# Two scatters a step instead of three while attention drains on GpSimd

## The reference

```
x = x + linear_attention(norm(x))      # 16 heads of 8, rotary
x = x + ffn(norm(x))                   # first mixture of experts
x = x + log_attention(norm(x))         # 16 heads of 8, causal
x = x + ffn(norm(x))                   # second mixture, same weights

log_attention:  L = q k^T / sqrt(8);  agg = sum_k(exp(clip(q ky^T / sqrt(8))) * mask)
                w = softplus(log(|L| + eps) - log(agg + eps)) * mask
                out = (w / (sum_k w + eps)) v @ w_proj^T
ffn:            shared expert on every token, plus the best 2 of 8 routed experts
                by sigmoid(x @ router + bias), weighted by the two normalised scores
```

## Time and profile before

| | us |
|---|---|
| median of 3 runs | 1026.67 (1026.3 to 1032.23) |
| the profiled execution | 1028.98 |
| its span | 1027.1 |
| busy in the span: PE / DVE / ACT / POOL | 819.4 / 735.8 / 568.5 / 586.9 |
| instructions of PE / DVE / ACT / POOL | 6459 / 1506 / 805 / 815 |
| mean granted clock of TensorE | 0.908 |

### The profile page before, as it was taken

One profiled execution on the slowest core, in us unless ns is written; L12 is line 12 of the kernel. 1 busy time (PEld: TensorE's weight loads), 2 busy tenths in 40 slices (PEclk: granted clock), 3 DMA queues, 4 the chain that ended last, 5 costly groups with the idle time before them and its releaser, 6 DMA issues. The chain is left out here.

```text
span 1027.1 us, 19542 instructions
## 1 busy us (share of the span) xinstructions
PE 819.4 (80%) x6459; PEld 545.3 (53%) x6459; DVE 735.8 (72%) x1506; ACT 568.5 (55%) x805; POOL 586.9 (57%) x815
## 2 busy tenths in 40 slices
PE   3887577899986787888888888979796588899890
PEld 2666566799984333333333333333342256799890
DVE  3888745455563658899999998989789646555574
ACT  1454152133334667989898989998763242233230
POOL 2343486881383666666644444455326877788884
PEclk9999588999997878999999999999877688999996
DMA  9990012123338477584737474732210021132444
GB/s 273 300 131 1 16 39 70 54 81 114 101 84 242 124 197 220 150 227 118 234 108 215 116 208 121 224 106 55 70 42 24 32 75 39 40 102 84 132 135 122
DMA packets 114401, 124.00 MB, mean 121 GB/s; under 512 B 13328, under 2 KB 76560, under 8 KB 114176
## 3 DMA queue, kind: packets, MB, share of 16 engines
q1 hardware_dynamic: 96512, 100.80, 36.2%
q0 software_dynamic: 8416, 17.29, 5.4%
q10 hardware_dynamic: 9376, 4.65, 1.6%
HBM read 59.97 MB, written 62.72 MB: 119 GB/s over the span
## 5 line engine op out<-in xcount | busy, mean ns | idle before, releaser
L2070 DVE TENSOR_SCALAR ring_b<-psum 128x1024 int32<-128x1024 int32 x160 | 194.2, 1216 | 24.0 <-PE psum L1765 20.8
L1930 ACT ACTIVATE ring_a<-psum 128x1024 f32<-128x1024 f32 x160 | 162.4, 1021 | 51.0 <-PE psum L1765 45.7
L1936 ACT ACTIVATE ring_b<-ring_b 128x1024 f32<-128x1024 f32 x160 | 168.7, 1055 | 36.5 <-DVE ring_b L2070 36.1
L2198 POOL TENSOR_SCALAR_AFFINE_SELECT ring_b<-ring_b 128x512 f32<-128x512 f32 (+1 forms) x112 | 80.1, 728 | 171.6 <-ACT ring_b L1936 170.9
L1765 PE MATMUL psum<-stacks 32*128 32x128 f32 (+3 forms) x1024 | 98.9, 385 | 66.2 <-DVE ring_b L2070 36.8
L1765 PEld LDWEIGHTS psum<-stacks 32*128 32x128 f32 x1024 | 56.9, 193 | 173.5 <-ACT ring_a L1930 76.6
L2062 DVE TENSOR_SCALAR ring_a<-ring_a 128x1024 f32<-128x1024 f32 x160 | 119.4, 751 | 16.8 <-ACT ring_a L1930 15.0
L949 ACT ACTIVATE ring_b<-psum 128x512 f32<-128x512 f32 x72 | 42.6, 591 | 114.0 <-PE psum L834 88.0
L1818 PE MATMUL psum<-ring_b,values 128*32 128x256 f32 (+3 forms) x1024 | 94.2, 478 | 8.6 <-POOL ring_b L2198 8.6
L1797 PE MATMUL psum<-ring_a,ones_s 128*32 128x256 f32 (+3 forms) x1024 | 92.3, 469 | 9.8 <-POOL ring_a L2198 9.8
L1092 POOL DMA_INDIRECT r_rows<-y_sorted,rows_of x64 | 67.1, 1048 | 51.3 <-DMA y_sorted<-y_out 39.2
(11 more groups left out here) (220 smaller groups left out, 1484.1 us busy)
## 6 DMA issues: line engine op xcount, KB each, us to landing
stack_q<-parts SPq DMA_DIRECT2D x32, 256.0 KB
stack_ky<-parts SPq DMA_DIRECT2D x32, 256.0 KB
stacks<-stack_q SPq DMA_DIRECT2D x64, 128.0 KB
stacks<-stack_ky SPq DMA_DIRECT2D x64, 128.0 KB
stack_k<-parts SPq DMA_DIRECT2D x32, 256.0 KB
stacks<-stack_k SPq DMA_DIRECT2D x64, 128.0 KB
stack_qr<-parts SPq DMA_DIRECT2D x32, 256.0 KB
stacks<-stack_qr SPq DMA_DIRECT2D x64, 128.0 KB
```

The lines of the kernel that those rows point to most:

```text
L1930: nc.scalar.activation(exps[:, n % RING, 2 * u:2 * u + 2, :], psum[:, first:first + 2, :], ACT.Exp, scale=SCALE).then_inc(self.exp, 1)
L1936: nc.scalar.activation(part, part, ACT.Ln, bias=1.0).then_inc(self.ln, 1)
L2070: nc.vector.tensor_scalar(ring[:, m % RING, HEADS_B[u][0]:HEADS_B[u][1] + 1, :].bitcast(I32), psum[:, first:first + 2, :].bitcast(I32), 0x ...
L2198: ins = nc.gpsimd.affine_select(out=part, in_=part, pattern=[[0, part.ap[1][1]], [1, 128]], compare_op=ALU.is_ge, fill=0.0, base=0, channe ...
```

## The change

In `lead_pool`, GpSimd's share of the drain for `ffn_2`: the first chunk's scatters go two a step in k = 10 to 16, and the remaining ten go in one piece in step 17. `mark_second`, which stands at scatter 12, thereby moves from step 14 to step 16. The inverse deviation of batch 8 moves from step 19 to step 20, behind three more scatters of the second chunk. The number of instructions on each engine stays.

```diff
                 if k == 15:
                     self.pool_rstd(p, self.first_late)
-                if 10 <= k < 18:
-                    self.send(p, 0, 3 * (k - 10), 3 * (k - 9))
-                if k == 19:
+                if 10 <= k < 17:
+                    self.send(p, 0, 2 * (k - 10), 2 * (k - 9))
+                if k == 17:
+                    self.send(p, 0, 14)
+                if k == 20:
                     self.pool_rstd(p, B)
                 if 18 <= k:
                     self.send(p, 1, 3 * (k - 18), 3 * (k - 17))
```

## The result

The changed kernel is slower by about 1%: 1040.44 us median against 1028.49 us, ratio 1.0096 with a 95% interval of 1.0073 to 1.0119, which is +7.5 to +12.2 us; the two medians by themselves stand at 1.0116, inside that interval. The forecast was +8.8 us. Executions of one kernel spread over some 12 us (1026.11 to 1038.52 before, 1036.07 to 1048.36 after), and most of that arises ahead of the drain: the drain's first scatter comes at 777.93 in the trace before and at 773.86 in the trace after, in code that is the same, and over all 13 traces of this document between 772.32 and 784.68. So traces are compared from that scatter on, and a time so counted is written R. The span then ends at R 249.2 before and R 261.5 after, +12.4 us.

A forecast was written before the change was run, and what follows sets the result against it. GpSimd was taken as the bound from the last mask on: its own +4.1 us, plus 2.3 waiting for first results, plus 2.4 of TensorE's clock, gave +8.8, 1035.5 us against the median of 1026.67; range 1029 to 1040.

The forecast's parts named there:

- What bounds the kernel before: From the last mask on GpSimd bounds the end; TensorE's side is early by only 2.5 us at the first quad.
- Part 1: Masks with two scatters a step: the last mask comes at 812.82, 2.84 us earlier.
- The shared port: GpSimd masks slow VectorE's two-input reads; two or three vanished collisions give 2.3 us, sum 6.5; not counted, 8.8 kept.
- Part 2: GpSimd alone, from the last mask to batch 8's moved deviation and the scatter behind it: +4.1 us.
- Part 3: VectorE's bias waits for batch 8's deviation, 8.9 us late, nothing absorbs it; GpSimd waits 2.3 us, end at +6.4.
- Part 4: TensorE's clock falls after idling some 13 us before 844.8: 2.4 us lost, bounds 0 and 5.6; end at +8.8.
- The sum: At the end: +8.8 us, 1037.8 us against the profiled execution, 1035.5 us against the median of 1026.67.
- SyncE's loads: Loads of the first four quads wait for the first chunk's landing, over 50 us before its results: no cost.
- the long clock loss: Rival: TensorE's clock stays low as long as after 816.35, 6.4 + 5.6 = +12.0 us, 1038.7 us; chance 0.18.
- The last mask is the bound: Rival at TensorE's 6.16 us wait at 816.35: the 2.84 us come through, faster, 1023.8 us; chance 0.10.
- Less is lost: Rival: port relief or slack behind the deviation; only GpSimd's +4.1 us, 1030.8, or +1.8 with relief; chance 0.16.
- a further slip: Rival: TensorE's delay meets late loads or the third chunk's rows, +15 us and more, 1042 us; chance 0.06.

The follow-up runs named there:

- e5: Kernel before with ten more pauses on GpSimd between its 64th scatter and the first result scatter; ratio to the kernel before 1.0042.
- e1: Changed kernel with batch 8's inverse deviation in step 18, right behind the first chunk's last scatter, instead of step 20; ratio to the kernel before 1.0015.
- e7: Changed kernel with VectorE's bias of batch 8 moved behind the product (`shared_hidden`) of the same round; ratio to the kernel before 1.0093.
- e8: Kernel before, three scatters a step, with batch 8's inverse deviation between the second and third scatters of step 19; ratio to the kernel before 1.0011.

## Why the prediction was right, point by point

- *What bounds the kernel before*: right, and shown by e5. The room that TensorE's side had at the first quad decided the size, since GpSimd's own delay was small. I had it 0.5 us too large: a result scatter starts 0.75 us behind ScalarE's copy, not 0.25, so the room was 2.0 us and not 2.5.
- *Part 1, last mask 2.8 us earlier*: 3.9 us. The variance of batch 7 was itself sooner by 1 us (803.19 + 0.17, R 29.5, against R 30.6), as were the logarithms.
- *The shared port*: this is where that 1 us comes from, and I had put the term at nothing. The second L1389 (L1391 after) took 1.68 us at R 4.66 beside a mask, and 0.74 at R 4.61 (778.47), where the mask, with one scatter fewer ahead of it, was already over. From there to batch 7's variance VectorE's instructions are 1.0 us earlier. All six traces in which that step holds three scatters show 1.68 there, and all seven with two show 0.74. So one collision vanished, for 0.94 us. Another only moved: L1351 took 1.08 us beside a mask at R 23.8 before and 0.17 after, but there L1344 and L1349 (L1346 and L1351) took 0.84 and 0.46 us beside a mask and a scatter, instead of 0.23 each. The two or three collisions of my other sum (2.3 us) would have been too many. What the 1 us was worth at the end was not measured by itself.
- *Part 2, GpSimd +4.1 us*: at the seventh scatter of the second chunk +3.5 (R 65.4 against R 61.9), at the 64th +1.9. The first of these is 0.6 us less than forecast: scatter 12 came 1.4 us sooner, mostly by the earlier mask, and the 18 slots behind it took 0.8 us more. Of the other 1.6 us, 0.9 fall between the marks of the second and third chunk, where the trace before has a scatter of 1.37 us and a gap of 0.98, and 0.7 behind the last mark, where before the scatters took up to 1.08 us while VectorE copied weights; after, the last of them was issued when the copies began. I had taken the rest of GpSimd's list as fixed.
- *Part 3, VectorE 8.9 us late, nothing absorbs it*: 8.3 us, and nothing did: TensorE's idle time behind the bias is 10.5 us, 10.3 before. e1 shows that most of the loss hangs on it, e7 that ScalarE's list holds the same work.
- *Part 4, the clock, 2.4 us*: this term was mis-sized. It measured 5.35 us (first results 66.46 us behind the bias against 61.11), near my upper bound of 5.6 but for another reason: two stretches at half rate, which cost 3.7 and 1.6 us. I had priced one by the fall at 851.5. In other executions with a long wait it was 3.8 us, still more than I took.
- *The sum*: first results +13.6 us instead of +11.3 (8.3 + 5.35, not 8.9 + 2.4). Less the room of 2.0 instead of 2.5 us that makes F +11.7 instead of +8.8, and the last scatter is +11.5. GpSimd is idle 9.97 us instead of 4.7. The timed runs say +7.5 to +12.2 us, so the forecast lies in the interval while the one trace lies 2.7 us above the forecast. Being wrong on GpSimd's own length by 2 us did no harm, for it was no longer what bounds: that was luck. The error on the clock went into the end in full. In absolute time the measured median is 1040.44 us against my 1035.5; 1.8 of the difference is that the kernel before had a median of 1028.49 over 17 executions and 1026.67 over the three I started from.
- *SyncE's loads*: at no cost, as said. The result scatters take 115.0 us from the first to the last, 115.1 before.
- *The rivals*: the long clock loss (+12.0) is what the profiled execution shows in size, though not by its mechanism. "The last mask is the bound" fell: the mask is 3.9 us earlier and the end later. "Less is lost" and "a further slip" did not happen.

## What to carry to other kernels

When an engine is the bound and its work is constant, count its idle time before and after: a change of order can only win what is idle now, here 3.5 us, and opened 6 us among the masks and 10 at the results. Look up, for each small thing that is delayed, what stands behind its consumer in that engine's list; here a 128x4 bias held a whole expert phase on two engines. What a long wait for another engine costs TensorE is the wait plus slower products behind it; to tell this from a longer chain, compare busy and idle time of the same instructions in both traces. So leave a few microseconds of spare time ahead of such a place, more than the same point moves from one execution to another.

## What the runs showed of the hardware

- The first down product behind a pause of TensorE, over eleven traces: 2.02 us after 2.32 to 2.52 us idle (four traces), 3.43 us after 4.43, 3.78 after 4.63, and 3.75 us after 6.06, 7.26, 9.54, 14.12 and 16.45. A longer pause made that product no slower than one of 6 us, and it took 1.95 us when added products filled the pause. The Trainium skill ("TensorE: Matmul & The Clock Gate", Part 1) calls throttled the default state, which activity releases. The changed kernel's trace agrees: TensorE was idle from 825.8, the granted clock fell from 0.99 to 0.50 at 831, and it was back at 0.98 in the window at 848, after 8 us of products. The second fall, to 0.50 in the window at 852, came with TensorE busy again behind a pause of 1.60 us.
- Executions of the same code reach the drain's first scatter between 772 and 785 us, and from there the variance of batch 8 between R 49.5 and R 52.5 with the changed masks. A place fitted to one trace was 2 us off in the next (e8).
- A VectorE instruction with two inputs (1x568, L1389) took 1.68 us beside a GpSimd mask of 1.09 us in six traces, and 0.74 us without one in seven.
- A result scatter of GpSimd that waited for ScalarE's copy started 0.75 us behind its end, in eight traces.
- A pause on GpSimd (memset and the wait for its end) took 0.42 us in a row of ten, and 0.61 us behind a scatter.
